# Softmax weights scaled before their transpose, and the second projection moved ahead of the weighing, in the score pass of a graph kernel

## What is computed

```python
D = jnp.abs(x[:, :, None, :] - x[:, None, :, :])
h = jnp.einsum('bijc,oc->bijo', D, W1) + b1
...                                     # batch norm over all pairs
h = _leaky(h)
s = jnp.einsum('bijo,uo->biju', h, W2)[..., 0] + b2[0]
s = jnp.where(A_init > 0, s, NEG)
A = jax.nn.softmax(s, axis=-1)
y = jnp.einsum('bij,bjc->bic', A, x)
y = y @ Wg.T + bg
...                                     # batch norm over all rows, leaky
out = jnp.concatenate([x, y], axis=2) @ Wt.T + bt
```

## Time and profile before

| | |
|---|---|
| Time, median of 3 | 2432.14 us (2431.3 to 2433.63) |
| Profiled execution | 2431.84 us, of which the span 2429.6 us |
| Busy over the span | PE 2016.0 us, DVE 2112.9 us, ACT 2236.6 us, POOL 46.6 us |
| DMA, in slices that lie within the score pass | 333 to 351 GB/s |

### The profile page before, as it was taken

The page is one execution under the profiler, slowest core; times in us unless marked ns, Lnnn a source line. Parts: engine busy times, 40 slices in busy tenths (PEclk is TensorE's granted clock), DMA queues, the critical chain, the costliest instruction groups (busy, mean ns, idle before and its releaser), DMA issues.

```text
span 2429.6 us, 35822 instructions
## 1 busy us (share of the span) xinstructions
PE 2016.0 (83%) x12869; PEld 800.9 (33%) x12869; DVE 2112.9 (87%) x2615; ACT 2236.6 (92%) x3468; POOL 46.6 (2%) x50
## 2 busy tenths in 40 slices
PE   5777767888888888888888888887888888889986
PEld 4555542323232333323232332322122222222225
DVE  5888868999999999999999999998988888888866
ACT  5999977999999999999999999997899999999985
POOL 0000000000000000000000000000000000000000
PEclk8999989999999999999999999999999999999997
DMA  4111105444444444444444444443999999999962
GB/s 116 40 43 44 40 18 176 169 172 173 167 178 167 178 167 177 166 173 166 177 167 174 171 169 173 167 172 139 351 349 343 339 333 339 333 339 340 339 232 70
DMA packets 230502, 470.48 MB, mean 194 GB/s; under 512 B 53496, under 2 KB 144312, under 8 KB 213944
## 3 DMA queue, kind: packets, MB, share of 16 engines
q1 hardware_dynamic: 229264, 467.84, 51.8%
q10 hardware_dynamic: 1064, 0.36, 0.1%
HBM read 254.19 MB, written 213.91 MB: 193 GB/s over the span
## 4 chain that ended last, share of the span: by engine, by line
ACT 35%; DVE 26%; issue 21%; PE 17%; DMA 1%; ACTq 0%; SPq 0%; POOLq 0%; POOL 0%; DVEq 0%
ACT banks L623 11%; PE banks L865 8%; DVE diff L1208 6%; DVE diff L1336 5%; ACT hcopy L620 5%; ACT habs L620 5%; ACT hcopy L644 4%; DVE ring L1080 4%; ACT habs L644 3%; PE banks L779 2%; ACT diff L608 2%; ACT diff L644 2%; DVE diff L1222 2%; PE banks L789 2%; DVE ring L1098 1%
## 5 line engine op out<-in xcount | busy, mean ns | idle before, releaser
L865 PE MATMUL banks<-diff,w1t 128*64 128x512 f32 x5136 | 1212.2, 603 | 192.6 <-ACT banks L623 141.9
L1208 DVE TENSOR_TENSOR diff<-ring 128x2048 f32<-128x2048 f32 x352 | 802.9, 2289 | 115.8 <-PE banks L865 115.8
L865 PEld LDWEIGHTS banks<-diff,w1t 128*64 128x64 f32 x5136 | 341.8, 137 | 927.5 <-issue 814.5
L623 ACT ACTIVATE banks<-banks,par 128x1024 f32<-128x1024 f32 x512 | 559.1, 1092 | 11.0 <-PE banks L865 8.5
L1222 DVE TENSOR_SCALAR diff<-diff 128x2048 int32<-128x2048 int32 x354 | 415.5, 1220 | 0.0
L1336 DVE TENSOR_TENSOR diff<-ring 128x2048 f32<-128x2048 f32 x128 | 299.9, 2343 | 8.1 <-PE banks L865 7.9
L608 ACT ACTIVATE diff<-banks 128x2048 f32<-128x2048 f32 x128 | 240.3, 1878 | 1.3 <-PE banks L880 1.3
L620 ACT ACTIVATE hcopy<-banks 128x1024 f32<-128x1024 f32 x192 | 197.0, 1026 | 18.4 <-PE banks L865 18.1
L620 ACT ACTIVATE habs<-banks 128x1024 f32<-128x1024 f32 x192 | 196.9, 1026 | 18.4 <-PE banks L865 18.1
L880 PE MATMUL banks<-pick,yt 32*128 32x256 f32 x2560 | 183.6, 401 | 1.0 <-ACT ring L591 1.0
L644 ACT ACTIVATE diff<-diff,par 128x2048 f32<-128x2048 f32 x86 | 180.7, 2101 | 0.5 <-DMA diff<-kept_two 0.5
(11 more groups left out here) (213 smaller groups left out, 1810.9 us busy)
## 6 DMA issues: line engine op xcount, KB each, us to landing
diff<-kept_two SPq DMA_DIRECT2D x86, 1024.0 KB, 6.7
kept_two<-hcopy SPq DMA_DIRECT2D x128, 512.0 KB, 2.6
kept_two<-habs SPq DMA_DIRECT2D x128, 512.0 KB, 2.6
hcopy<-kept_two SPq DMA_DIRECT2D x42, 1024.0 KB, 6.8
kept_one<-hcopy SPq DMA_DIRECT2D x64, 512.0 KB, 2.6
kept_one<-habs SPq DMA_DIRECT2D x64, 512.0 KB, 2.6
hcopy<-kept_one SPq DMA_DIRECT2D x64, 512.0 KB, 6.9
habs<-kept_one SPq DMA_DIRECT2D x64, 512.0 KB, 7.1
```

The lines of the kernel that those rows point to most:

```text
L623: nc.scalar.activation(h, h, ACT.Square, bias=par[:, 53:54], accum_out=column(SQUARES + c)).then_inc(sq_done, 1)
L865: last = nc.tensor.matmul(dst[half * O:(half + 1) * O, bank * BANK:(bank + 1) * BANK], w1t[:, :], src[:, m * BANK:(m + 1) * BANK], start=T ...
L1208: v.tensor_tensor(shaped(diff[:, c % ND, :]), xj, xi_, ALU.subtract).then_inc(sub_done, 1)
```

## The change

Batch b's weights are now normalised before they are transposed, so the aggregate needs no scaling behind it. The rows are projected by Wg first, one step group ahead (`project_rows`, PE), and bg is added as they are taken from PSUM (`take_rows`, DVE); as the weights of a row sum to one, adding bg to the rows is the same as adding it to y. Then y comes from two matmuls with 256 columns (`weigh_rows`), with channels on partitions, and neither the transposed aggregate nor the copy `aggt` exists any more. ACT's `y_out` becomes a plain copy. The steps move too: `masked` from kk 6 to 5, `add_upper` from kk 5 to 4, `y_out` from (b+4, kk 2) to (b+3, kk 5), `y_statistics` from (b+4, kk 3) to (b+3, kk 6); `LAST` shrinks by 5 steps. The load of bg becomes a broadcast to all partitions (`bgb`) in place of one column of `par`.

```diff
-    LAST = B * PAIRS + 28
+    LAST = B * PAIRS + 23
...
+            sp.dma_start(bgb[:, :], bg.rearrange("(a n) -> a n", a=1).to_broadcast([P, C])).then_inc(par_loaded, 16)
...
-            def aggt_out(b):
-                act.wait_ge(aggt_ready, b + 1)
-                nc.scalar.activation(aggt[:, :], agp, ACT.Copy).then_inc(aggt_copied, 1)
-
             def y_out(b):
                 act.wait_ge(y_ready, b + 1)
-                nc.scalar.activation(bass.AP(yt, b * N, [[B * N, P], [1, N]]), yp, ACT.Identity,
-                                     bias=par[:, 5:6]).then_inc(y_copied, 1)
+                nc.scalar.activation(bass.AP(yt, b * N, [[B * N, P], [1, N]]), yp, ACT.Copy).then_inc(y_copied, 1)
...
-                if kk == 7 and 3 <= b <= B + 2:
-                    aggt_out(b - 3)
-                if kk == 2 and 4 <= b <= B + 3:
-                    y_out(b - 4)
+                if kk == 5 and 3 <= b <= B + 2:
+                    y_out(b - 3)
...
+            def project_rows(b):
+
+                if b >= 2:
+                    pe.wait_ge(y_copied, b - 1)
+                for t in range(NT):
+                    off = b * RING + t * WRAP
+                    last = nc.tensor.matmul(xgp[:, t * C:(t + 1) * C], ring[:, off:off + P], wgt[:, :], start=True, stop=True)
+                last.then_inc(xg_ready, 1)
+
             def transpose_probs(b):
-                pe.wait_ge(prob_ready, b + 1)
+                pe.wait_ge(prob_scaled, b + 1)
...
+            def weigh_rows(b):
                 pe.wait_ge(probt_copied, b + 1)
...
+                pe.wait_ge(xg_added, min(b + 2, B))
+                for jt in range(NT):
+                    last = nc.tensor.matmul(yp, bass.AP(yt, b * N + jt * C, [[B * N, P], [1, C]]), probt[:, jt, :],
+                                            start=(jt == 0), stop=(jt == NT - 1))
+                last.then_inc(y_ready, 1)
...
-            def normalise_agg(b):
+            def scale_probs(b):
                 dve.wait_ge(prob_ready, b + 1)
                 v.reciprocal(small[:, 6:8], small[:, 4:6]).then_inc(den_ready, 1)
-                dve.wait_ge(agg_ready, b + 1)
                 dve.wait_ge(den_ready, b + 1)
                 for t in range(NT):
-                    last = v.tensor_scalar(agg[:, t, :], agp[:, t * C:(t + 1) * C], small[:, 6 + t:7 + t], None, ALU.mult)
-                last.then_inc(agg_copied, 1)
+                    last = v.tensor_scalar(prob[:, t, :], prob[:, t, :], small[:, 6 + t:7 + t], None, ALU.mult)
+                last.then_inc(prob_scaled, 1)
+
+            def take_rows(b):
+                dve.wait_ge(xg_ready, b + 1)
+                v.tensor_tensor(bass.AP(yt, b * N, [[B * N, P], [C, NT], [1, C]]), xgp.rearrange("p (t c) -> p t c", t=NT),
+                                bass.AP(bgb, 0, [[C, P], [0, NT], [1, C]]), ALU.add).then_inc(xg_added, 1)
...
+                if kk == 4 and 2 <= b <= B + 1:
+                    add_upper(b - 2)
                 if kk == 5 and 2 <= b <= B + 1:
-                    add_upper(b - 2)
-                if kk == 6 and 2 <= b <= B + 1:
                     masked(b - 2)
-                if kk == 5 and 3 <= b <= B + 2:
-                    normalise_agg(b - 3)
-                if kk == 3 and 4 <= b <= B + 3:
-                    y_statistics(b - 4)
+                if kk == 0 and 3 <= b <= B + 2:
+                    scale_probs(b - 3)
+                if kk == 6 and 3 <= b <= B + 2:
+                    y_statistics(b - 3)
+                if kk == 1 and 2 <= b <= B + 1:
+                    take_rows(b - 2)
```

More of the change, by code:

```diff
@@ L104, in gnn_pair_kernel @@
         btb = sb("btb", [P, C])
+        bgb = sb("bgb", [P, C])
         small = sb("small", [P, 64])
@@ L131, in gnn_pair_kernel @@
         agg = sb("agg", [P, NT, C])
-        aggt = sb("aggt", [P, N])
         tokeep = [hcopy[:, q, :] for q in range(4)] + [habs[:, q, :] for q in range(4)]
@@ L162, in gnn_pair_kernel @@
         ppt = ps[3][:, 0:BANK]
-        agp = ps[3][:, BANK:BANK + 256]
+        xgp = ps[3][:, BANK:BANK + 256]
         yp = ps[3][:, BANK + 256:2 * BANK]
@@ L259, in gnn_pair_kernel @@
         probt_copied = sem("probt_copied")
[L260 to L263, removed]
+        prob_scaled = sem("prob_scaled")
+        xg_ready = sem("xg_ready")
+        xg_added = sem("xg_added")
         y_ready = sem("y_ready")
@@ L348, in _ @@
             sp.dma_start(par[:, 4:5], b2.rearrange("(a n) -> a n", a=1).to_broadcast([P, 1])).then_inc(par_loaded, 16)
-            for col, v in ((5, bg), (6, gg), (7, beg)):
+            for col, v in ((6, gg), (7, beg)):
                 sp.dma_start(par[:, col:col + 1], v.rearrange("(n a) -> n a", a=1)).then_inc(par_loaded, 16)
@@ L964, in transpose_probs @@
                 last.then_inc(probt_ready, 1)
-            def aggregate(b):
+            def weigh_rows(b):
                 pe.wait_ge(probt_copied, b + 1)
[L968 to L974, removed]
-                last.then_inc(agg_ready, 1)
-            def transpose_agg(b):
-                pe.wait_ge(agg_copied, b + 1)
-                for t in range(NT):
-                    last = nc.tensor.transpose(agp[:, t * P:(t + 1) * P], agg[:, t, :], ident[:, :])
-                last.then_inc(aggt_ready, 1)
-            def second_projection(b):
-                pe.wait_ge(aggt_copied, b + 1)
-                nc.tensor.matmul(yp, wgt[:, :], aggt[:, :], start=True, stop=True).then_inc(y_ready, 1)
+                pe.wait_ge(xg_added, min(b + 2, B))
[3 more added lines that the diff above has]
+                last.then_inc(y_ready, 1)
             again(0)
@@ L997, in _ @@
                     scores(b - 2)
-                if kk == 0 and 3 <= b <= B + 2:
+                if kk == 1 and 3 <= b <= B + 2:
                     transpose_probs(b - 3)
                 if kk == 3 and 3 <= b <= B + 2:
-                    aggregate(b - 3)
-                if kk == 5 and 3 <= b <= B + 2:
-                    transpose_agg(b - 3)
-                if kk == 0 and 4 <= b <= B + 3:
-                    second_projection(b - 4)
+                    weigh_rows(b - 3)
+                if kk == 0 and 2 <= b <= B + 1:
+                    project_rows(b - 2)
             def output(g):
```

## The result

The changed kernel takes 2415.18 us (median of 4, 2413.01 to 2418.21) against 2431.72 us before; the ratio is 0.9933 with a 95% interval of 0.9919 to 0.9947. It is faster, by 0.7% and clear of the noise, but by 16.5 us instead of 38.5, and lies outside the range of 2388 to 2404.

The account below looks back on a forecast made before the run. The prediction took ACT and DVE, each waiting for the other once per 20.50 us period, as the bound. Its terms, 25.9 + 7.3 + 2.3 + 5.0 - 2.0 = 38.5 us, off 2431.8 gave 2393 us, range 2388 to 2404.

Parts of the forecast that it names:

- The waits for the row maximum: ACT's exponentials waiting for DVE's negated row maximum: all 27 waits go with masked moved earlier, 25.9 us gained.
- the cause that I had named second: On DVE: the wait at y_statistics for ACT's y, 1.79 us a period, ends because y_out is two steps ahead.
- `aggt` and `y_out`: On ACT: dropping the aggt copy gains 7.3 us, y_out as a plain copy 2.3; period 19.18 us.
- DVE: New scalings and take_rows make DVE's work 19.07 us a period, range 18.91 to 19.31, just within ACT's 19.18.
- Rival 1: DVE becomes the bound, costing up to 6 us; time 2396 to 2399; chance 0.14.
- PE: Tensor engine has fewer passes and one wait less, is not the bound; no change of the time.
- rival 3: ACT's wait moves to the fresh chunk or transposed weights, leaving 14.6 us gain, time 2417; chance 0.06.
- rival 4: Slower: take_rows waits for PE in DVE's queue, deciding above 1.43 us; time 2457 at 2.5 us; chance 0.04.
- rival 5: Rescheduling without effect: masked waits for the transposed scores at its new place; 2431 to 2425; chance 0.03.
- SP and DMA: SP's program nearly unchanged; traffic rises to 362 GB/s, share 0.98; 2.0 us given back, bounds 0 and 12.
- Rival 2: The DMA queue becomes the bound, showing waits for kept chunks in most periods; time 2403; chance 0.15.
- Behind the last batch: Tail after the last scores: nothing changes up to GpSimd's masking, the shorter chain behind it gains 5.0 us.

Follow-up runs that it names:

- e9: Kernel before with add_upper at kk 4, masked at kk 5, and in SP's queue store_scores at kk 6, load_adj2 at kk 7; 2405.57 us.
- e2: Kernel before with only add_upper moved to kk 4 and masked to kk 5, old arithmetic and old queue; 2420.96 us.
- e12: Changed kernel with store_scores at kk 6, load_adj2 at kk 7, and add_upper and masked put back to kk 5 and 6; 2391.67 us.
- e7: Changed kernel with load_blocks reading the previous batch's stored scores, so SP does not wait for the landing, DMAs kept; 2387.09 us.
- e8: Changed kernel with store_scores at kk 6 of SP's queue and load_adj2 at kk 7, swapped from 7 and 6; 2390.08 us.
- e11: Changed kernel with store_scores left at kk 7 behind the 1 MB load, and load_adj2 moved behind it; 2389.69 us.
- e10: Kernel before with only the swap in SP's queue, store_scores at kk 6 and load_adj2 at kk 7; 2433.24 us.
- e4: Changed kernel with the DMAs of load_blocks issued by GpSimd ahead of mask_blocks instead of by SP; 2393.97 us.
- e1: Changed kernel with load_blocks issued two steps later in SP's queue, at kk 4 instead of kk 2; 2430.67 us.

## Why the prediction was wrong

**The waits for the row maximum.** Right: all 27 are gone. The size was a little low. In e9, whose ACT work is that of the kernel before, the period is 19.39 us instead of 20.50: 1.11 us for a wait that the trace shows as 0.97, the lost overlap again. The cause I gave for their going, `masked` ahead of the subtraction, was only one of two that suffice: the move alone does it (e2, e9), and so do the new arithmetic with the earlier `y_out` and `y_statistics` (e12). DVE's wait for y, 42.9 us from 1800 to 2300 us before, does not occur in that window of e12, which fits the cause that I had named second.

**`aggt` and `y_out`.** Right: 0.26 us for the copy. ACT's period of 19.18 was 0.15 us too long. Where nothing stalls it is 19.03 us (e7, e8, e11), the figure that the early period of the earlier trace rows had given; I had taken the wait off the period at its shown 0.97. That ACT is busy 19.17 us in the period shown under Result is no confirmation of 19.18, because the wait in it breaks an overlap. In e7 the pass from ACT's first chunk to its last takes 38.9 us less than before, against 35.5 in the sum.

**DVE.** Right. The scaling of 128x256 takes 0.351 us (mean of 64; bounds 0.29 and 0.43), `take_rows` 0.42, and in e8 DVE is busy 489.57 of 500 us, 97.9% against 98% expected. Its wait for `project_rows` was 12.5 us over the whole pass, and ACT waited for no chunk because of it. Rival 1 did not occur.

**PE, rivals 3 to 5.** From 1800 to 2300 us of the changed kernel ACT waits neither for a fresh chunk nor for the transposed weights (rival 3), DVE's waits at `take_rows` are 1.1 us at the longest, where rival 4 needed more than 1.43 in each period, and `masked` does not wait for the transposed scores (rival 5).

**SP and DMA: here it failed.** The step reads "SP's program is the same", turns to GB/s, and gives back 2.0 us with a bound of 12. The chunks came late for 19.9 us in the pass, and with the lost overlaps the pass took 23.9 us more than in e7. That SP's program is unchanged was true and beside the point. It holds a chain whose parts do not get shorter with the period, and the prediction put this chain at nothing: copy of the scores, store, its landing, the seven loads of the scores, and only then the kept chunk of kk 3. One such chain in the kernel before, on SP and ACT:

```profile
2014.56 0.58 ACT L664 ACTIVATE sring<-banks 128x512 f32<-128x512 f32 x1
2015.17 1.72 SPq L427 DMA_DIRECT2D ring_scores<-sring  x4
2022.04 0.58 SPq L440 DMA_DIRECT2D ub<-ring_scores  x1
2027.20 0.60 SPq L414 DMA_DIRECT2D hcopy<-kept_two  x1
2036.37 2.11 ACT L644 ACTIVATE hcopy<-hcopy,par 128x2048 f32<-128x2048 f32 x1
```

In the kernel before, for the copies from 1800 us on, this chunk was issued 11.5 to 14.1 us behind the copy, landed 5.0 to 6.2 us later and was wanted 7.7 to 10.3 us after its issue, so 2 to 5 us were to spare. In the changed kernel it is issued 15.0 to 17.1 us behind the copy, lands 5.0 to 8.0 us later, and ACT takes it within 0.5 us of its landing. ACT wanted the chunk 21.8 us behind the copy before, and wants it 20.0 us behind it where nothing stalls (e7, e8). So the shorter period takes 1.8 us of the room, and the later landing of the stores (8.3 us, before 5.7), which are also issued up to 1.8 us later, takes the rest. I had weighed the engines' throughput against the demand and not this chain's length against the period.

The sign was in the trace of the kernel before. The one wait of 0.5 us of the earlier trace rows, which I put down to buffers being filled, was at the end of this very chain, behind the short first period of 17.3 us; the chunk was issued at 1744.97 and landed 5.8 us later:

```profile
1750.77 2.09 ACT L644 ACTIVATE diff<-diff,par 128x2048 f32<-128x2048 f32 x1 [0.50 <-DMA diff<-kept_two]
```

Behind the period of 19.03 us of the earlier trace rows (copy at 1789.06) 1.1 us were left to spare. The share of 0.91 in the changed kernel refutes the limit by throughput: the DMA engines were less busy than in the earlier trace rows, while ACT waited for them. Rival 2 named the right resource, and the sign that it gave, waits for kept chunks in most periods, came (21 in 500 us), but its mechanism was wrong, and so was its price: the 345 GB/s came from the period with the 0.5 us wait.

One bound does not follow from its own terms either: with nothing given back and the tail at its best the sum gives 2390, not 2388. Nothing hangs on it.

The Trainium skill, "DMA: Bandwidth & Descriptors", says two things that bear on this. In "Two DMAs through the same engine are not ordered" it says that within one queue of one DMA engine descriptors start in order; the landing of a 32 KB store after 8.3 us behind a burst and 3.0 us ahead of it agrees with that. The 358 GB/s of its Specifications, which I had weighed in the prediction, do not bind here: 363 GB/s over 500 us in e8.

**Behind the last batch.** From the end of ACT's last chunk to the last statistics (the start of L1405, L1412 before) it is 24.5 us, predicted "some 22", before 27.3:

```profile
2341.41 1.54 SPq L421 DMA_DIRECT2D adjt<-in_adj_dram  x3
...
2343.00 1.81 SPq L427 DMA_DIRECT2D ring_scores<-sring  x4
...
2351.99 0.72 POOL L509 TENSOR_TENSOR ub<-ub,band 128x256 f32<-128x256 f32 x1 [8.39 <-DMA ub<-ring_scores]
...
2355.69 0.50 ACT L672 ACTIVATE prob<-adjt,small 128x256 f32<-128x256 f32 x1
...
2362.68 1.01 DVE L1405 BATCH_NORM_AGGREGATE small<-row_stat 128x2 f32<-128x192 f32 x1
```

From GpSimd's masking (its end at 2352.71) to the statistics it is 9.97 us against 14.85, 4.9 gained where 5.0 were predicted. But I had written that nothing changes ahead of it, and 2.1 us were lost there: SP came to the last store only at 2343.00, 2.6 us behind the start of the copy (0.7 before), since `load_blocks` and the adjacency stood ahead of it. The same step failed, in the same queue.

**Where the 42 us of the best versions come from.** Each part of the change alone or with the queue mended: the new place of `masked` with the old queue 12 us (e2), with the mended queue 27 (e9); all of the change with the old queue 16.5, with the mended queue 42 to 43 (e8, e11). The queue's edit alone is worth nothing (e10). So the new arithmetic and its places bring 15.5 us on top of e9 (2405.57 to 2390.08), of which the sum of the prediction explains 9.6 for `aggt` and `y_out` and 3 to 5 for the tail.

The versions that beat both kernels are the changed kernel with the store of the scores ahead of the adjacency loads (e8 and e11), 2390.1 and 2389.7 us. e7, which reads the scores of the batch before and so spares the wait, is 3 us faster than e8. By the two traces only 0.7 us of that lie between ACT's first chunk and its last, 1.5 behind the last chunk, where e7 does not wait for the last store, and 0.9 in the output, which nothing here explains.

**Left open.** Whether the late store and the late burst really repeat each other was not shown: e7 shows that the standing delays the stores, but e11 can be had from the shorter chain alone. How the time of single executions spreads in e4 (2388 to 2403) and in e1 (2414 to 2436) was not traced; e1's median is 16 us above its profiled execution, so its trace names the stall and not its full size. Why two periods of over 21 us come in a row in the changed kernel (2242.69 to 2285.69) was not looked into; in both of them the store was issued 2.4 us behind the copy instead of 0.9.

## What to carry to other kernels

When a kernel is made faster, go through every chain of fixed length that spans a period (copy, store, landing, reload, the transfer queued behind it) and hold its length against the new period, even in programs that the change does not touch. A wait for a DMA's landing in a queue that also feeds the bounding engine is the first place to look; put what is waited for ahead of bulk transfers. Measure the queue by when the prefetches behind the wait are issued and when they are wanted, not by GB/s, and not by how long the queue stands in all: SP stands 189.3 us of 500 in the changed kernel and 182.2 us in e8, which is 25 us faster. What counts is where it stands. A pair of waits that hold each other up, as DVE and ACT did, can hide such a chain nearly completely.

## What the runs showed of the hardware

How long a 32 KB store took to land depended on the order and the time of the issues on one queue, at nearly the same total traffic per period: 8.3 us behind a burst of 4 MB, 6.5 us with the three small loads taken from ahead of it (e11), 3.0 us ahead of the adjacency and of the kk 7 load (e8), and 5.6 us in the old order where the queue did not stand for the landing (e7).

The DMA engines carried 360 to 363 GB/s for 500 us with ACT waiting 1 us or less (e4, e7, e8, e11). The DMA share was no measure of what was left: it was 0.95 in e11 and 1.00 in e8 at 361 and 363 GB/s.

A wait on ACT cost some 0.13 us more than its shown length, because the instruction ahead of it no longer overlapped the next (0.42 us for a wait of 0.29).

In e7, where ACT never rests in the window, its rows are longer but their starts are no farther apart: a row of 2048 columns, `diff`, takes 2.44 us on average in the pass of e7 and 2.10 in that of the changed kernel, and from its start to the next start it is 1.99 us in e7 and 2.00 in the changed kernel. The cost of such a row is read from the starts.
